# Attention and a routed expert layer on one core: bodies written out, smaller reloads of the input, block numbering moved, and another operand for the second bias

## What is computed

```python
xn = _layernorm(x, axis=-1)
s = _L0_attn_ref(xn, W_qkv, W_out)       # scores + slope * (k - q), causal softmax, @ v, @ W_out
g = _silu(_L0_ffn_ref(xn, gate_w, gate_b, w1, b1, w2, b2))
x = x + s * g
# in _L0_ffn_ref:
gate_logits = x @ gate_w + gate_b
topk_vals, topk_idx = jax.lax.top_k(gate_logits, 2)
topk_w = jax.nn.softmax(topk_vals, axis=-1)
h = gelu(einsum('btd,edf->ebtf', x, w1) + b1)
y = einsum('ebtf,efd->ebtd', h, w2) + b2
output = einsum('ebtd,bte->btd', y, comb)   # comb: topk_w at the two chosen experts
```

## Time and profile before

| | |
|---|---|
| median of 3 runs | 1212.18 us (1210.99 to 1213.15) |
| profiled execution, span | 1211.8 us |
| PE busy | 1128.9 us, 93% |
| DVE busy | 988.1 us, 82% |
| ACT busy | 936.6 us, 77% |
| POOL busy | 888.1 us, 73% |
| instructions | 51694 |
| transfers | 148.74 MB, mean 123 GB/s |

### The profile page before, as it was taken

The page is one execution under the profiler, slowest core; times in us unless marked ns, Lnnn a source line. Parts: engine busy times, 40 slices in busy tenths (PEclk is TensorE's granted clock), DMA queues, the critical chain, the costliest instruction groups (busy, mean ns, idle before and its releaser), DMA issues.

```text
span 1211.8 us, 51694 instructions
## 1 busy us (share of the span) xinstructions
PE 1128.9 (93%) x16970; PEld 834.2 (69%) x16970; DVE 988.1 (82%) x3099; ACT 936.6 (77%) x1835; POOL 888.1 (73%) x1064
## 2 busy tenths in 40 slices
PE   2668999999999999999999998999999999999996
PEld 1446767677777777777888766677777777777775
DVE  7687898888888888885777867788888888888883
ACT  3547878888888888886666677788888888888884
POOL 6069989898888888885000077788888888888896
PEclk9989999999999999999999999999999999999998
DMA  8424765556555555555335337655555555555553
GB/s 259 161 54 105 135 125 133 128 131 134 128 130 127 127 129 127 130 133 99 86 84 123 76 79 163 129 128 122 123 123 122 121 122 125 125 121 122 122 125 74
DMA packets 267956, 148.74 MB, mean 123 GB/s; under 512 B 173154, under 2 KB 256450, under 8 KB 267204
## 3 DMA queue, kind: packets, MB, share of 16 engines
q1 hardware_dynamic: 263476, 138.72, 51.8%
q0 software_dynamic: 4096, 8.40, 2.5%
q10 hardware_dynamic: 272, 0.13, 0.0%
HBM read 15.76 MB, written 16.78 MB: 27 GB/s over the span
## 4 chain that ended last, share of the span: by engine, by line
PE 63%; POOL 16%; issue 6%; DVE 3%; ACT 2%; SPq 2%; DMA 2%; POOLq 0%; ACTq 0%; DVEq 0%
POOL t_lo L829 11%; PE ps L998 10%; PE ps L904 7%; PE ps L970 6%; PE ps L905 6%; PE ps L906 6%; PE outs L1030 5%; PE ps L1002 5%; PE outs L1034 5%; PE outs L1032 4%; PE ps L999 3%; PE ps L1007 2%; ACT stage L1299 2%; PE outs L905 1%; PE outs L904 1%
## 5 line engine op out<-in xcount | busy, mean ns | idle before, releaser
L829 POOL TENSOR_TENSOR t_lo<-stage 128x512 f16<-128x512 f32 x640 | 651.8, 1037 | 121.5 <-ACT stage L1299 120.0
L1592 DVE CUSTOM_DVE_ANT_0 stage<-ps,kmask 128x512 bf16<-128x512 f32 (+3 forms) x1024 | 451.4, 488 | 113.5 <-PE ps L970 98.6
L1299 ACT ACTIVATE stage<-ps,slope 128x512 f32<-128x512 f32 (+1 forms) x768 | 439.5, 617 | 91.5 <-PE ps L1007 79.5
L998 PE MATMUL ps<-q_st,k_st 128*128 128x256 f16 (+3 forms) x1024 | 299.8, 303 | 9.2 <-issue 5.0
L1030 PE MATMUL outs<-v_sp,stage 128*128 128x65 f16 x2560 | 264.6, 195 | 7.9 <-POOL t_lo L829 6.4
L1032 PE MATMUL outs<-v_sp,stage 128*128 128x64 f16 x2560 | 263.3, 194 | 0.0
L1034 PE MATMUL outs<-v_sp,t_lo 128*128 128x65 f16 x2560 | 263.1, 194 | 0.0
L1030 PEld LDWEIGHTS outs<-v_sp,stage 128*128 128x128 bf16 x2560 | 235.4, 98 | 32.1 <-issue 14.2
L1032 PEld LDWEIGHTS outs<-v_sp,stage 128*128 128x128 bf16 x2560 | 235.7, 99 | 0.0
L1034 PEld LDWEIGHTS outs<-v_sp,t_lo 128*128 128x128 f16 x2560 | 235.4, 98 | 0.0
L999 PE MATMUL ps<-q_st,k_st 128*128 128x128 f16 x1024 | 223.9, 219 | 0.0
(11 more groups left out here) (218 smaller groups left out, 2672.3 us busy)
## 6 DMA issues: line engine op xcount, KB each, us to landing
q_st<-stage SPq DMA_DIRECT2D x256, 128.0 KB, 2.4
k_st<-stage SPq DMA_DIRECT2D x128, 128.0 KB
q_st<-stage SPq DMA_DIRECT2D x256, 64.0 KB, 2.0
k_st<-stage SPq DMA_DIRECT2D x128, 64.0 KB
slot_y<-stage SPq DMA_DIRECT2D x40, 128.0 KB, 2.1
X<-in_L_attn_inputs SPq DMA_DIRECT2D x8, 512.0 KB, 6.6
slot_x<-att SPq DMA_DIRECT2D x2, 2048.0 KB, 8.8
wx_raw<-in_L_ffn_w SPq DMA_DIRECT2D x64, 64.0 KB
```

Of the source, the lines that this page charges most:

```text
L829: pool.tensor_tensor(t_lo[r], t_p[r], upper(t_p[r]), ALU.subtract).then_inc(s[f"lo{u % NG}"], 1)
L998: pe.matmul(d, k[:, 0, at], q[:, 0, seen], start=(c0 == 0), stop=False, skip_group_check=True)
L1299: e = act.activation(t_p[r][:, c0:c1], S_ps[u % 2][:, c0:c1], ACT.Exp, scale=slope[:, bass.ds(pair_index(n) * 2 * SLOTS + sl * 2 + h, 1)])
L1592: ins = dve.tensor_tensor_reduce(junk[h][:, c0:c0 + w], M_ps[h][:, c0:c0 + w], kmask[:, SEQ - w:SEQ], -1.0 / 1024, 3e38, ALU.add, ALU.min, ...
```

## The change

- run_bodies writes out every window; no engine has a loop in its bodies any more. TWICE becomes (4, 9, 14), and the second send of such a window comes one window later for each of its two transfers.
- inputs_again becomes a task X0 in SP's table of the second half, between H0 and Q1; in even windows it loads two tiles (128 KB), sixteen times in all. POOL's last step for a pair waits for that pair's transfer instead of all four.
- route(6) and route(7) stand behind N1 of body 30 and A1 of body 30. The comparison, its sum and the block numbers are on one partition. Its result lies in a piece of the buffer stage, and the scratch for the other steps is a buffer of its own.
- b2 is loaded as eight rows, twice (partitions 0 to 7 and 32 to 39), and its high and low parts are made before the first body. pick holds for each expert a matrix that is 1 in rows e and 32 + e and 0 elsewhere; it takes the place of the ones as the stationary operand, and b2_rows is the same for all experts. PE waits for it once, before the first expert block.

```diff
-            ("A0", -1, 2), ("Q0", 1, 33), ("K0", 2, 51), ("A1", -1, 60), ("H0", -4, 60), ("Q1", 1, 76), ("K1", 2, 93),
+            ("A0", -1, 2), ("Q0", 1, 33), ("K0", 2, 51), ("A1", -1, 60), ("H0", -4, 60), ("X0", 0, 61), ("Q1", 1, 76), ("K1", 2, 93),
...
-                              ("N0", 5), ("N0", 8), ("A1", HALF - 1)],
+                              ("N1", HALF - 2), ("A1", HALF - 2), ("A1", HALF - 1)],
...
-        def run_bodies(eng, engine_name, tasks, lo, hi):
-
-
-            start, end = lo + (max(TWICE) + UNROLL if lo == 0 else 2 * UNROLL), hi - (2 * UNROLL if lo == 0 else UNROLL)
-            for w in range(lo, start):
-                one_window(engine_name, tasks, w, lo, hi, w)
-            with eng.Fori(start // UNROLL, end // UNROLL) as i_:
-                for c in range(UNROLL):
-                    one_window(engine_name, tasks, i_ * UNROLL + c, lo, hi, c)
-            for w in range(end, hi):
+        def run_bodies(engine_name, tasks, lo, hi):
+
+            for w in range(lo, hi):
                 one_window(engine_name, tasks, w, lo, hi, w)
...
-        FIRST_SENT, TWICE = 2, (4, 7, 10)
+        FIRST_SENT, TWICE = 2, (4, 9, 14)
...
-            def inputs_again(c):
-
-                sp.dma_start(X[:, 8 * c:8 * c + 8, :], xt[:, 8 * c:8 * c + 8, :]).then_inc(s["xend"], 16)
+            def inputs_again(n, par, _):
+
+                if par == 0:
+                    t = n - HALF
+                    sp.dma_start(X[:, t:t + 2, :], xt[:, t:t + 2, :]).then_inc(s["xend"], 16)
...
+            pick_step(pool.memset(pick[:, :, :], 0.0))
+            for row in (0, 32):
+                pick_step(pool.affine_select(out=pick[:, :, :], in_=pick[:, :, :], compare_op=ALU.not_equal, fill=1.0,
+                                             base=-row, pattern=[[-1, E], [0, P]], channel_multiplier=1))
+            pool.wait_ge(s["sm"], 80)
+            pool.wait_ge(s["consts"], 9)
+            for row in (0, 32):
+                v = b2_in[row:row + E, :]
+                pick_step(pool.tensor_scalar(v, v, WS, 1.0, ALU.mult, ALU.mult))
+                pick_step(pool.tensor_copy(b2_rows[row:row + E, :], v))
+            lo = b2_rows[32:32 + E, :]
+            pool.tensor_tensor(lo, b2_in[32:32 + E, :], lo, ALU.subtract).then_inc(s["b2"], 1)
+            pool.wait_ge(s["b2"], 1)
...
-                name, body = FIRST_ONES["POOL"][k + O_STEPS]
-                group_done(pool, "lo", body, int(name[1:]))
-                if k == 4:
-                    lo = b2_row[32:33, :, :]
-                    ins = pool.tensor_tensor(lo, b2v[32:33], lo, ALU.subtract)
-                elif k % 2 == 0:
-                    ins = pool.tensor_scalar(v, v, WS, 1.0, ALU.mult, ALU.mult)
-                else:
-                    ins = pool.tensor_copy(b2_row[row:row + 1, :, :], v)
...
-                    pool.wait_ge(s["xend"], 64)
+                    pool.wait_ge(s["xend"], pairs * 16)
...
-                    pe.matmul(y.rearrange("p (t d) -> p t d", d=D), ones[:, :],
-                              b2_row[:, bass.ds(e, 1), :].to_broadcast([P, BT, D]), start=True, stop=False,
+                    pe.matmul(y.rearrange("p (t d) -> p t d", d=D), pick[:, bass.ds(e, 1), :].rearrange("p a q -> p (a q)"),
+                              b2_rows[:, :].unsqueeze(1).to_broadcast([P, BT, D]), start=True, stop=False,
...
-                    small(dve.tensor_tensor(ended, block_no[:, :, :], end.unsqueeze(1).to_broadcast([P, NBLK, E]), ALU.is_ge))
+                    small(dve.tensor_tensor(ended, block_no[:, :].unsqueeze(2).to_broadcast([1, NBLK, E]),
+                                            end[0:1, :].unsqueeze(1).to_broadcast([1, NBLK, E]), ALU.is_ge))
```

More of the change, by code:

```diff
@@ L256, in build @@
         t_p = [piece(i) for i in (0, 1, 2, 3, 6)]
+        ended = piece(10)[0:1, 0:NBLK * E].rearrange("p (b e) -> p b e", e=E)
         junk = [piece(10).bitcast(BF16)[:, h * SEQ:(h + 1) * SEQ] for h in range(2)]
@@ L606, in _ @@
             enter_bodies("SP", {**stacks, "W": load_weights}, 0, HALF)
-            run_bodies(sp, "SP", {**stacks, "W": load_weights}, 0, HALF)
+            run_bodies("SP", {**stacks, "W": load_weights}, 0, HALF)
             def load(j, b):
@@ L662, in hand_out_or_leave @@
                     hand_out(n, par, 0)
[L664 removed]
+            run_bodies("SP", {**stacks, "H": hand_out_or_leave, "X": inputs_again}, HALF, BODIES)
             leave_bodies("SP", stacks, HALF, BODIES)
@@ L723, in _ @@
                       allow_small_or_imprecise_dtypes=True).then_inc(s["consts"], 1)
-            pool.memset(b2_row[:, :, :], 0.0).then_inc(s["consts"], 1)
+            pool.memset(b2_rows[:, :], 0.0).then_inc(s["consts"], 1)
             pool.memset(half[:, :], 0.5)
@@ L801, in send @@
             def send(n, par, k):
-                sent = [(t, at) for t, at, _ in sent_with(n, par) if (k, at) != (1, UNROLL)]
-                if k == 1 and isinstance(n, int) and n - 1 in TWICE:
-                    sent.append(sent_with(n - 1, 0)[0][:2])
+                sent = [(t, at) for t, at, _ in sent_with(n, par) if at != UNROLL]
+                if n - 1 - k in TWICE:
+                    sent.append(sent_with(n - 1 - k, 0)[0][:2])
                 for t, at in sent:
@@ L854, in _ @@
             enter_bodies("POOL", sends, 0, HALF)
-            run_bodies(pool, "POOL", {**sends, "Y": in_between}, 0, HALF)
+            run_bodies("POOL", {**sends, "Y": in_between}, 0, HALF)
             leave_bodies("POOL", sends, 0, HALF)
@@ L889, in _ @@
             enter_bodies("POOL", fetches, HALF, BODIES)
-            run_bodies(pool, "POOL", fetches, HALF, BODIES)
+            run_bodies("POOL", fetches, HALF, BODIES)
             leave_bodies("POOL", fetches, HALF, BODIES)
@@ L1110, in _ @@
             enter_bodies("PE", {**tasks, "Y": ranks}, 0, HALF)
-            run_bodies(pe, "PE", tasks, 0, HALF)
+            run_bodies("PE", tasks, 0, HALF)
             leave_bodies("PE", tasks, 0, HALF, late=LATE_O)
@@ L1212, in _ @@
             pe.wait_ge(s["yout"], NBLK)
-            run_bodies(pe, "PE", tasks, HALF, BODIES)
+            run_bodies("PE", tasks, HALF, BODIES)
             leave_bodies("PE", tasks, HALF, BODIES)
@@ L1361, in _ @@
             act.wait_ge(s["consts"], 9)
-            run_bodies(act, "ACT", {**tasks, "W": weights_hi, "R": send_hi}, 0, HALF)
+            run_bodies("ACT", {**tasks, "W": weights_hi, "R": send_hi}, 0, HALF)
             leave_bodies("ACT", {**tasks, "W": weights_hi, "R": send_hi}, 0, HALF)
@@ L1429, in weigh_other @@
                     weigh(n, par, k)
-            run_bodies(act, "ACT", {**tasks, "F": weigh_other, "T": gates, "Y": weigh_first}, HALF, BODIES)
+            run_bodies("ACT", {**tasks, "F": weigh_other, "T": gates, "Y": weigh_first}, HALF, BODIES)
             leave_bodies("ACT", {**tasks, "F": weigh}, HALF, BODIES)
@@ L1673, in _ @@
             dve.wait_ge(s["zeros"], 16 * ZERO_DMAS)
-            run_bodies(dve, "DVE", {**tasks, "Y": lambda k: route(k - CHOICES)}, 0, HALF)
+            run_bodies("DVE", {**tasks, "Y": lambda k: route(k - CHOICES)}, 0, HALF)
             leave_bodies("DVE", {**tasks, "Y": lambda k: route(k - CHOICES)}, 0, HALF, late=LATE_O)
@@ L1703, in _ @@
                 begin_half("DVE", tasks, HALF, BODIES, fill_part(STEPS - 1, STEP - 1, g))
-            run_bodies(dve, "DVE", tasks, HALF, BODIES)
+            run_bodies("DVE", tasks, HALF, BODIES)
             leave_bodies("DVE", tasks, HALF, BODIES, late=[BODIES - 1])
```

60 lines of the change are left out of this document (27 added, 33 removed).

## The result

The changed kernel takes 1190.15 us in the median of its runs, the kernel before 1212.56 us beside it; the ratio is 0.982, 95% interval 0.9801 to 0.9839. Run again later, beside three of the experiments, it gave 1189.65 against 1211.68 us and the same ratio. The profiled execution has a span of 1189.1 us (its run time 1190.88), 22.7 less than before.

The account below looks back on a forecast made before the run. TensorE (PE), 63% of the chain of waits, was taken as the bound. Terms -4.0 - 8.4 - 8.3 - 4.0 + 0.5 - 3.0 = -27.2 us from span 1211.8 gave 1184.6, forecast 1185 (67%), own range 1181 to 1190, with rivals to 1196.

Parts of the forecast that it names:

- second loop: Second half's 24 looped windows written out: 370.81 us against 15.10 us a window, gain 8.4 us, low end 4.
- numbering: Block numbering moved out of windows 5 and 8: 3.9 us gained, 0.9 given back in window 31, net 3.0.
- reload: Reload of X as sixteen 128 KB transfers instead of four of 512 KB: 8.8 us less 0.5, gain 8.3.
- Second bias: Five preparing operations leave POOL's bodies 0 and 1, so window 2 shortens: gain 4.0 us (3 to 4.3).
- The 0.5 us at the start: New bias preparation before body 0 can hold up VectorE's short chain for tile scales: cost 0.5 us (0 to 2).
- Double sends: Second sends moved from windows 4, 7, 10 to 4, 9, 14: zero (-0.7 to +0.7 us).
- First loop: First half's 16 looped windows written out, 15.38 to 15.13 us each: gain 4.0 us (3.5 to 4.5).
- slower rival: Code supply: about 100 instruction packets sit before stack transfers; 0.27 us each cancels the gain, 0.4 gives 1225 us; 3%.
- The 7.8 us: Gain from writing out both loops if each of 19 taken back edges cost only 0.41 us, instead of 12.4.
- (a): Second half: POOL and its chain through ACT keep windows at 15.3 us or more; time 1190 to 1193; 14%.
- (b): Small reloads delay every even window's q_st stack by an issue of 0.58 us, 9 us in all; time 1194; 8%.
- (c): Windows 2, 5 and 8: the next POOL or DVE wait ends as late; up to 7 us back, 1192; 8%.

## Why the prediction was right, and where it was not

The time, 1190.15 us, lies 5 us over the forecast of 1185 and at the upper edge (0.15 us over) of its own range of 1181 to 1190, inside the range to 1196. Of the terms of the sum all but the second loop hold within 1 us in this profile. That the total comes so near is in part luck: the second loop gave 5.5 us less than forecast and the expert stage took 2.4 us more, while windows 32 and 33 gave 1.7 that nobody forecast, and the numbering 0.9 and the reload 0.4 more than forecast. Nor do the parts stand by themselves: with the loops written out alone, windows 34 to 37 fall from 69.2 to 63.7 us already, with all four large reloads still in them.

**Reload**: 8.3 forecast, 8.7 us found in windows 34 to 37; 7.8 with the loop kept, 4.8 to 5.8 when undone in the changed kernel, and only 3.2 between the kernel that is merely written out and the changed one (63.7 against 60.5 us). The term isn't one number: a large transfer holds PE by as much as the key or query issue behind it is late for other reasons, and these wander. The small ones cost 0 to 0.5. The rule of the Trainium skill (SBUF — State Buffer, The DMA setup-cost knee), few large transfers, is for transfers that are themselves the bound; nobody waits for these twelve more, and the runs show no loss.

**Second bias**: 4.0 forecast, 4.3 found. The size is right, the reason half so: I put the gain on the move ahead of body 0, and the run with the operations moved back shows that their shape made nearly all of it. The 0.5 us at the start lies in the noise (windows 0 and 1: +0.4, and -0.6 in the second profile of the same kernel).

**Numbering**: 3.9 forecast, 3.9 found and 3.6 when undone, though when undone windows 5 and 6 have 3.6 of it and window 8, now without a double send, only 0.5 to 0.8. The 0.9 to be given back in window 31 didn't come, since the gap of 1.72 us ahead of the low part was in fact free for it.

**Double sends**: nothing, as forecast. The window behind one has 15.53 us wherever it stands (windows 6, 11, 16).

**First loop**: 4.0 forecast, 3.1 found; a double send lies in the stretch now (0.4), and two windows have bumps of 0.5 and 0.2.

**Second loop**: 8.4 forecast, 2.85 found in this profile and 4.9 in the mean of nine (370.9 less 366.0). This is the step that failed, and in two places. First, I took 15.10 as the level of all 24 windows from two pieces; from window 37 on the odd ones take 15.20 in every kernel with the loop gone, and window 40 takes 15.42 or 15.43 in all nine of these profiles, with a wait of PE of 0.26 us there, in the changed kernel for DVE. So an undisturbed stretch has 12 x 15.09 + 12 x 15.20 + 0.3 = 363.8 us, not 362.4. Second, the packets: 0.6 to 4.2 us over that level, 2.2 in the mean. The prediction had this mechanism as its slower rival, with 100 packets and 0.27 us each as the point from which it decides. There are 77 more, and if all that is over the level is theirs, each of the 49 in the stretch costs PE 0.01 to 0.09 us. The mechanism was real, the price a sixth of what decides (0.045 in the mean), because few packets hit a stack that has no time left: 36 long issues in this profile against 6 waits of PE ahead of a rough product, 2.8 us in all. Each of the six ends within 0.1 us of the landing of a key stack. Ahead of four of them, 1.4 us together, the transfer took 1.9 to 2.5 us and had been issued late, behind long issues; into the other two, 1.26 and 0.19 us, a packet falls while the stack's transfer is under way. What is shown is that the long issues and the waits for stacks come with PE's packets and go with them; that all that is over the level is due to packets is argued.

The Trainium skill's rule in the prediction (Runtime: NRT & Kernel Launch, Instruction fetch mechanics) had two halves. A taken branch out of the small window stalls for a fetch: with PE alone looped, 12 back edges cost 5.2 us, 0.43 each, but only one packet is fetched in that stretch, so these waits aren't such fetches, and no run here shows one. The 7.8 us that I had worked out from the earlier trace rows for both loops would have been the better term (3.1 and 4.9 found). Sequential fetch is hidden: for PE itself yes, its written-out windows run at 15.10; for SP's queue and the transfers beside it the measurement says no.

**Not forecast**: the expert stage takes 149.1 us instead of 146.7, and 147.6 to 150.9 in the twelve other runs. Of its code only the bias product's operands changed, and without that change, with the loops alone written out, it takes 148.5 already. In the changed kernel a packet of 0.89 us starts at 559.4, between the issue of the second load and PE's wait for it, where the kernel before has none. The records of all runs bear this out. Counted from C0 of window 31, the load is issued at 18.6 us in every kernel. PE waits for it 0.20 us in the kernel before, whose next packet starts at 22.1; 0.42 with a packet from 18.0; 0.9 to 1.2 in the five profiles with one from 19.4; and 1.6 to 2.0 in the four with one from 20.0 or 20.1. Of the three with one from 18.2, two wait 0.6 and one, whose packet lasts 1.53 us, 1.8. So most of the 2.4 us goes with where a packet falls. Rivals (a), (b) and (c) fell: POOL's chain has no floor at 15.3, even windows aren't the long ones, and windows 2, 5 and 8 are short.

## What to carry to other kernels

The price of a hardware loop is read from the waits at its back edges (here 12 x 0.43 us), and a total against two good windows overstates it; what takes the loop's place, the packets of straight code, is a load on the queues and their transfers and not on the engine that runs the code. Before an issue is moved on a queue that is busy for three quarters of the time (77% of the 24 windows here), look up who waits for its source to be read, not only who reads its destination: swapping two stacks for the sake of the second cost 20 us through the first. And when a preparation is in the way, change its shape before its place: 1024 elements in a row on one partition took 1.04 us, the same on eight partitions 0.29.

## What the runs showed of the hardware

A DMA issue on SP takes 0.6 us in the median (1.3 for a transposing one), but in the changed kernel up to 2.3 us (2.6) while a 16 KB packet of PE's instructions is under way. Of the 384 long issues in the 24 windows of all eleven profiles with the second half written out, 381 overlap one (packets cover 15 or 16% of the time); 8 KB packets of another queue, of which the kernel with PE alone looped still has 27 in the stretch, lengthen none. A key stack's transfer with such a packet under way lands 2.6 to 3.4 us after its issue (medians of the eleven profiles), one without 1.8 to 1.9. What in the chip ties them together no trace here shows.

The 24 windows of one and the same kernel took 367.96 and 366.31 us in two profiles, with the long windows in other places. So a single profile of written-out code can't price a change of 2 us in such a stretch.
